# Wide cross attention on one core: the two halves of each head's queries stacked along the contraction, and the engines' order taken from a list schedule

## What is computed

```python
# x: (2, 1024, 256); context: (2, 154, 192); Wq (256, 1024), Wk, Wv (192, 1024), Wo (1024, 256), bo (256,)
n = layernorm(x)
q, k, v = n @ Wq, context @ Wk, context @ Wv      # split in 16 heads of 64
x = x + softmax(q @ k.T / 8) @ v @ Wo + bo
```

## Time and profile before

| | |
|---|---|
| median of 3 runs | 1483.45 us (1481.06 to 1484.49) |
| the profiled execution | 1474.6 us, its span from first to last instruction 1472.8 us |
| mean granted PE clock | 0.95 of full |
| busy over the span | PE 89%, PEld 70%, DVE 69%, ACT 60%, POOL 32% |
| the wide cross attention's block | 367 to 652 us of the span |

### The profile page before, as it was taken

The page is one execution under the profiler, slowest core; times in us unless marked ns, Lnnn a source line. Parts: engine busy times, 40 slices in busy tenths (PEclk is TensorE's granted clock), DMA queues, the critical chain, the costliest instruction groups (busy, mean ns, idle before and its releaser), DMA issues. The chain is left out here.

```text
span 1472.8 us, 27606 instructions
## 1 busy us (share of the span) xinstructions
PE 1311.2 (89%) x9707; PEld 1036.3 (70%) x9707; DVE 1016.0 (69%) x1992; ACT 877.4 (60%) x2193; POOL 465.7 (32%) x636
## 2 busy tenths in 40 slices
PE   5989999988699999968999766689989699999997
PEld 3534444435699999856888644478877599999995
DVE  5688787816456665555777896678875588888773
ACT  4436676674466666544121466477872588888873
POOL 5312221238233333432000356422110234444320
PEclk9999999999999999988999887599998799999998
DMA  4745224000000000021000300021202567777855
GB/s 88 225 77 155 45 53 76 6 5 1 30 2 1 2 2 1 2 93 29 1 1 1 81 16 1 22 56 42 50 16 76 176 215 230 236 233 231 232 161 184
DMA packets 97922, 116.16 MB, mean 79 GB/s; under 512 B 23552, under 2 KB 83193, under 8 KB 97785
## 3 DMA queue, kind: packets, MB, share of 16 engines
q1 hardware_dynamic: 88329, 99.84, 25.1%
q0 software_dynamic: 4416, 12.06, 2.7%
q10 hardware_dynamic: 5040, 2.49, 0.7%
HBM read 88.48 MB, written 16.55 MB: 71 GB/s over the span
## 5 line engine op out<-in xcount | busy, mean ns | idle before, releaser
L827 ACT ACTIVATE sa_probs<-ps 128x512 f32<-128x512 f32 (+1 forms) x304 | 154.3, 578 | 84.3 <-PE ps L780 83.2
L851 DVE TENSOR_REDUCE sa_top<-ps 128x2 f32<-128x1024 f32 (+3 forms) x160 | 171.4, 1115 | 37.7 <-PE ps L756 24.2
L3150 ACT ACTIVATE room<-ps,cx_top 128x154 f32<-128x154 f32 x256 | 97.2, 389 | 89.8 <-DVE cx_top L3214 89.8
L2688 PE MATMUL ps<-me_h,me_w_parts 128*128 128x256 f32 x1104 | 141.4, 289 | 4.2 <-DVE me_h L2774 4.2
L2688 PEld LDWEIGHTS ps<-me_h,me_w_parts 128*128 128x128 f32 x1104 | 138.0, 194 | 5.9 <-DVE me_h L2774 4.8
L2702 PE MATMUL ps<-me_w_parts,me_mid 128*128 128x256 f32 x1104 | 136.3, 283 | 0.0
L2702 PEld LDWEIGHTS ps<-me_w_parts,me_mid 128*128 128x128 f32 x1104 | 132.5, 188 | 0.0
L3012 POOL TENSOR_TENSOR room<-room 128x512 f32<-128x512 f32 x64 | 66.7, 1043 | 169.9 <-DVE room L3222 169.8
L2769 DVE TENSOR_TENSOR me_w_parts<-me_chunk,me_w_parts 128x1024 fp32r<-128x1024 f32 x92 | 110.4, 1222 | 13.2 <-ACT me_w_parts L2730 13.2
L2753 ACT ACTIVATE me_full<-ps,me_b 128x256 f32<-128x256 f32 x184 | 95.2, 517 | 40.5 <-PE ps L2688 40.5
L2798 DVE TENSOR_TENSOR me_mid<-me_full,me_mid 128x256 fp32r<-128x256 f32 x184 | 90.1, 507 | 41.3 <-ACT me_mid L2755 39.2
(11 more groups left out here) (472 smaller groups left out, 3437.0 us busy)
## 6 DMA issues: line engine op xcount, KB each, us to landing
me_chunk<-in_L_ffn_W_dram SPq DMA_DIRECT2D x92, 512.0 KB, 4.0
sa_k<-scr_k SPq DMA_DIRECT2D x48, 128.0 KB, 4.2
sa_q<-scr_q SPq DMA_DIRECT2D x96, 64.0 KB, 4.0
cn_qd<-cn_qh SPq DMA_DIRECT2D x60, 64.0 KB, 2.1
scr_q<-room SPq DMA_DIRECT2D x6, 512.0 KB, 4.3
scr_k<-room SPq DMA_DIRECT2D x6, 512.0 KB, 4.7
me_b<-in_L_ffn_b_dram SPq DMA_DIRECT2D x23, 128.0 KB, 4.3
x<-in_x_dram SPq DMA_DIRECT2D x4, 512.0 KB, 6.3
```

What stands on the lines that cost most here:

```text
L827: act.activation(probs[:, step % self.PROBS, h0:h0 + many, 0:w], src[:, :, 0:w], ACT.Exp, scale=DH ** -0.5).then_inc(exped.sem, 1)
L851: dve.tensor_reduce(top2[:, k % 2, k0 // 512, h0:h0 + many, sb % HBLK], src[:, :, 0:w], AX.X, ALU.max).then_inc(freed.sem, 1)
L2688: last = pe.matmul(ps[:, MID + n % 4, 0:RT], w[:, u % 2, 0, i, DM * k + P * b:DM * k + P * b + P], h[:, u % 2, j, k, :], start=(m == 0), s ...
L3150: last = act.activation(p[:, h + i, :], ps[:, S_BANK + n % SR, M * i:M * i + M], ACT.Exp, bias=top[:, t % 2, h + i:h + i + 1], accum_out=d ...
```

## The change

The query parts of two heads are no longer the stationary operand together. After each round, four DMAs of 128 KB from SP copy `cx_qh` and `cx_ql` into a new buffer `qq`, where a head owns 128 partitions: its high part in one half and its low part in the other. The keys of a head stand in both halves of `kh` and `kl`; `project_out` fills the second half by eight DMAs of 308 KB from SP, in two sets of four, and the memsets to zero go. `scores` has then two matmuls of 154 columns a head (with kh and with kl; low times low comes in too), four for a group of two heads. `qh` and `ql` shrink to one round, so `high_q` and `low_q` of a round wait for the copies of the round before. `xh` and `xl` shrink to one pair. `load_ffn` comes behind the copies of the first pair on SP. The order of PE, ACT, DVE and POOL comes from `order()`, which places each step at the earliest start by a table of durations. What `weigh`, `turn`, `output` and `exp` compute is as before.

```diff
+                for i in range(2):
+                    for keys, name in ((cross.kh, k_high), (cross.kl, k_low)):
+                        sp.wait_ge(name.sem, name.at(MB // 2 * (i + 1)))
+                        for a in range(2):
+                            own, other = W * a, W * (1 - a)
+                            part = lambda at: raw(keys[at:at + W, H // 2 * i:H // 2 * (i + 1), :, :]).rearrange(
+                                "p (m a) b k -> p a m (b k)", a=2)[:, a, :, :]
+                            sp.dma_start(part(other), part(own)).then_inc(cross.k_set[i].sem, 16)
...
-                pool.memset(cross.kh[:, :, :, :, :].bitcast(F32), 0.0).then_inc(k_zero.sem, 1)
-                pool.memset(cross.kl[:, :, :, :, :].bitcast(F32), 0.0).then_inc(k_zero.sem, 1)
...
-                act.wait_ge(k_zero.sem, k_zero.at(1))
                 for m in range(MB):
                     act.wait_ge(kmm.sem, kmm.at(m + 1))
                     for j in range(HB):
-                        last = act.activation(cross.kh[W * j:W * j + W, :, m, j, :],
+                        last = act.activation(cross.kh[W * j:W * j + W, HB * m + j, :, :],
...
-                dve.wait_ge(k_zero.sem, k_zero.at(2))
...
-        self.kh = sb("kh", [P, B, self.blocks, self.hb, M], F32R)
-        self.kl = sb("kl", [P, B, self.blocks, self.hb, M], F32R)
+        self.kh = sb("kh", [P, H, B, M], F32R)
+        self.kl = sb("kl", [P, H, B, M], F32R)
+        self.k_set = [c.own_sig(f"{name}k_set{i}") for i in range(2)]
...
+    def order(self):
+
+
+        ns, act_turns, turns = self.ns, (1, 3), self.TURNS
+        work, last = {}, {}
+
+        def add(item, engine, span, after):
+            kind = item[0], engine
+            work[item] = engine, span, after + ([last[kind]] if kind in last else [])
+            last[kind] = item
+
+        for t in range(NT):
+            add(("normal", t, 0), "DVE", 0.4, [("turn_x", t // 2 - 2, 0)] if t >= 4 else [])
+            add(("bias", t, 0), "POOL", 0.75, [("normal", t, 0)])
+            for s in range(ns):
+                after = [("exp",) + divmod(ns * t + s - 3, ns)] if ns * t + s >= 3 else []
+                if t % PAIR == 0:
+                    after.append(("laid", t // PAIR, s // 2))
+                add(("scores", t, s), "PE", 0.31, after)
+                add(("highest", t, s), "DVE", 0.41, [("scores", t, s)])
+                add(("exp", t, s), "ACT", 0.74, [("highest", t, s)] + ([("norm", t - 1, s // 2)] if t else []))
+            for q in range(QUADS):
+                add(("inverse", t, q), "DVE", 0.1, [("exp", t, 2 * q + 1)])
+                add(("norm", t, q), "POOL", 1.4, [("inverse", t, q)] + ([("turn", t - 2, 4)] if q == 0 and t >= 2 else []))
+            for i in range(5):
+                n = 5 * t + i - 2
+                after = [("norm", t, min(turns[i], 3))] + ([("turned",) + divmod(n, 5)] if n >= 0 else [])
+                if t:
+                    after.append(("weigh", t - 1, 0 if i < 2 else 1))
+                add(("turn", t, i), "PE", 0.43, after)
+                add(("turned", t, i), "ACT" if i in act_turns else "DVE", 0.5 if i in act_turns else 0.6, [("turn", t, i)])
+            for r in range(2):
+                after = [("turned", t, i) for i in ((0, 1, 2) if r == 0 else (3, 4))]
+                if t or r:
+                    after.append(("low_o", t, 0) if r else ("low_o", t - 1, 1))
+                if t:
+                    after.append(("output", t - 1, r))
+                add(("weigh", t, r), "PE", 2.0, after)
+                add(("high_o", t, r), "ACT", 0.5, [("weigh", t, r)])
+                add(("low_o", t, r), "DVE", 0.6, [("high_o", t, r)])
+                add(("output", t, r), "PE", 1.42, [("low_o", t, r)] + ([("add", t - 1, 0)] if t and r == 0 else []))
+            add(("add", t, 0), "DVE", 0.85, [("output", t, 1), ("bias", t, 0)])
+        for g in range(NPAIR):
+            add(("turn_x", g, 0), "PE", 0.43, [("normal", t, 0) for t in (2 * g, 2 * g + 1)]
+                + ([("low_q", g - 1, 3)] if g else []))
+            add(("high_x", g, 0), "ACT", 0.5, [("turn_x", g, 0)])
+            add(("low_x", g, 0), "DVE", 0.6, [("high_x", g, 0)])
+            for r in range(4):
+                add(("queries", g, r), "PE", 1.42, [("low_q", g, r - 1) if r else ("low_x", g, 0)])
+                before = [("laid",) + divmod(4 * g + r - 1, 4)] if g or r else []
+                add(("high_q", g, r), "ACT", 0.5, [("queries", g, r)] + before)
+                add(("low_q", g, r), "DVE", 0.6, [("high_q", g, r)])
+                add(("laid", g, r), "SP", 3.8, [("low_q", g, r)] + ([("scores", 2 * g - 3, 2 * r + 1)] if g >= 2 else []))
+        hop = {"PE": 0.24, "DVE": 0.17, "ACT": 0.17, "SP": 0.0, "POOL": 0.3}
+        ahead = {}
+
+        def path(item):
+
+            if item not in ahead:
+                engine, span, _ = work[item]
+                ahead[item] = span + max([path(x) + (0.03 if work[x][0] == engine else hop[engine]) for x in next_of[item]],
+                                         default=0.0)
+            return ahead[item]
+
+        next_of = {item: [] for item in work}
+        for item, (_, _, after) in work.items():
+            for a in after:
+                next_of[a].append(item)
+        for item in reversed(list(work)):
+            path(item)
+        free, end, items = dict.fromkeys(hop, 0.0), {}, []
+        while work:
+            best = None
+            for item, (engine, span, after) in work.items():
+                if all(a in end for a in after):
+                    start = max([free[engine]] + [end[a][0] + (0.03 if end[a][1] == engine else hop[end[a][1]]) for a in after])
+                    key = start - 0.005 * ahead[item]
+                    if best is None or key < best[0]:
+                        best = key, start, item
+            _, start, item = best
+            engine, span, _ = work.pop(item)
+            free[engine] = start + span
+            end[item] = start + span, engine
+            items.append((engine, item))
+        return items
...
-        xh = sb("xh", [P, 2, KD, TOK], F32R)
-        xl = sb("xl", [P, 2, KD, TOK], F32R)
-        qh = sb("qh", [P, 2, MB, TOK], F32R)
-        ql = sb("ql", [P, 2, MB, TOK], F32R)
+        xh = sb("xh", [P, KD, TOK], F32R)
+        xl = sb("xl", [P, KD, TOK], F32R)
+        qh = sb("qh", [P, 2, TOK], F32R)
+        ql = sb("ql", [P, 2, TOK], F32R)
+        qq = sb("qq", [P, 2, H, TOK], F32R)
...
-        V_AT = ((4, 0, 0), (7, 0, 1)) if wide else ((0, 1, 0),)
-        OUT_AT = ((2, 1, 1), (6, 0, 0)) if wide else ((3, 1, 0),)
-        ADD_AT = 3 if wide else 4
-        Q_AT = (2, 6) if wide else (3,)
...
-                weights.load_ffn(sp)
+                for g in range(NPAIR):
+                    for r in range(QR):
+                        if g >= 2:
+                            sp.wait_ge(s_s.sem, s_s.at(NS * (PAIR * g - 3) + 2 * r + 2))
+                        for src, swap, name in ((qh, 0, s_qh), (ql, 1, s_ql)):
+                            sp.wait_ge(name.sem, name.at(QR * g + r + 1))
+                            for a in range(2):
+                                at = 64 * (a ^ swap)
+                                dst = raw(qq[at:at + 64, g % 2, 4 * r:4 * r + 4, :]).rearrange("p (m a) n -> p a m n", a=2)
+                                sp.dma_start(dst[:, a, :, :], raw(src[64 * a:64 * a + 64, :, :])).then_inc(s_laid.sem, 16)
+                    if g == 0:
+                        weights.load_ffn(sp)
...
-                    m, h, hn = groups[s]
+                    _, h, hn = groups[s]
                     b, g, i = t // ST, t // PAIR, t % PAIR
-                    if s == 0 and i == 0:
-                        pe.wait_ge(s_ql.sem, s_ql.at(QR * g + QR))
+                    if t == 0 and s % (NS // 2) == 0:
+                        half = self.k_set[s // (NS // 2)]
+                        pe.wait_ge(half.sem, half.at(16 * 4))
+                    if i == 0:
+                        pe.wait_ge(s_laid.sem, s_laid.at(64 * (QR * g + s // 2 + 1)))
                     if n >= SR:
                         pe.wait_ge(s_exp.sem, s_exp.at(n - SR + 1))
-                    j = h - HB * m
-                    for k, (a, v) in enumerate(((qh, self.kh), (ql, self.kh), (qh, self.kl))):
-                        last = pe.matmul(ps[:, S_BANK + n % SR, 0:M * hn], a[:, g % 2, m, P * i:P * i + P],
-                                         v[:, b, m, j:j + hn, :], start=(k == 0), stop=(k == 2))
+                    for j in range(hn):
+                        for keys in (self.kh, self.kl):
+                            last = pe.matmul(ps[:, S_BANK + n % SR, M * j:M * j + M], qq[:, g % 2, h + j, P * i:P * i + P],
+                                             keys[:, h + j, b, :], start=(j == 0 and keys is self.kh),
+                                             stop=(j == hn - 1 and keys is self.kl), skip_group_check=True)
...
```

(56 more changed lines are left out.)

176 lines of the change are left out of this document (55 added, 121 removed).

## The result

| | kernel before | changed kernel |
|---|---|---|
| median of 4 runs each | 1482.45 us (1481.06 to 1484.49) | 1472.9 us (1472.02 to 1473.29) |
| ratio, 95% interval | | 0.994 (0.992 to 0.996) |
| the profiled execution, its span | 1474.6, 1472.8 us | 1473.29, 1471.6 us |
| first key product to last output, in the profiles | 351.67 to 649.79 = 298.12 us | 354.12 to 645.71 = 291.59 us |

The changed kernel is 9.5 us faster. The two profiled executions differ by only 1.3 us, because that of before was some 8 us faster than its own timed runs.

What follows compares the result with a forecast made beforehand. PE's work was taken to bound the steady part. Scores +1.0, order -2.9, head +3.5, tail -4.0 and boundary +1.0 summed to -1.4 us, from 1483.45 to 1482; likeliest 1475 to 1490, whole range 1462 to 1492.

Steps and rivals of the forecast that it cites:

- the planner's entry: Order's duration table: a group of scores has 0.31 us where 0.45 was expected; said to do PE no harm.
- The bound: Steady part, tiles 2 to 14: PE's work sets the time, 16.02 us per tile, 0.33 of it gaps.
- Scores: Score matmuls on PE: weight loads set the pace, 0.113 us each; +0.06 us per tile, +1.0 in all (-1.3 to +6.6).
- Rival 1: Score matmuls: columns set the pace, 0.07 us each, 1.19 us less per tile; whole 1462 us; chance 0.22.
- The order: Steady part: the list schedule closes gaps, leaving 0.15 us per tile; -2.9 us in all (0 to -5.3).
- Copies: Query copies: landing in 2.3 us, a round taking 4.8 us, hidden in the steady part.
- The head term: Start of the block: first scores earlier, but pair 0's last queries later through the copy chain; +3.5 us (0 to +6).
- The tail: End of the block: better order cuts PE's idle time, 14.6 us chain instead of 18.9; -4 us (-6 to 0).
- The boundary: Before the first scores: last key copies issued after the last reciprocal, memsets' removal no gain; +1.0 us (+0.3 to +1.3).
- Rival 2: Query copies are the bound: landing takes 4.2 us, a round 6.8, delaying pairs 0 and 1; +10, 1492 us; chance 0.18.
- rival 3: Steady part: the order closes no gaps, which stay at 0.33 us per tile; +2.9, 1485 us; chance 0.08.
- The likeliest case: Whole kernel: the forecast's own terms together, -1.4 us (-8 to +7), 1482 us within 1475 to 1490; chance 0.52.

Runs made afterwards that it cites:

- e6: e5 plus waits: a round's split waits for the previous round's copies, scores for their tile's copies, and the order is planned with these waits; 1473.1 us, ratio 0.9939.
- e5: e1 plus the four 128 KB query copies per round, into a buffer nobody reads; 1462.8 us, ratio 0.9873 to the kernel before.
- e11: The changed kernel, unedited, timed again on another occasion; 1476.44 us, ratio 0.9969 to the kernel before.
- e1: The kernel before with only the list-scheduled order and two finer waits, without new products or copies; 1464.5 us, ratio 0.9885.
- e9: The changed kernel with the dropped, unused 32 bytes per partition (`bq`) allocated again; 1474.02 us, ratio 0.9952 to the kernel before.
- e10: e1 with the unused 32 bytes per partition (`bq`) left out; 1464.61 us, ratio 0.9893 to the kernel before.
- e8: The changed kernel with 0.45 instead of 0.31 us for a group of scores in the planner's table; 1472.56 us, ratio 0.9937.
- e7: The changed kernel with two buffers for split queries instead of one, and next-stage weights loaded after the last copy; 1470.76 us, ratio 0.9926.
- e3: The changed kernel with score products over 128 instead of 154 columns, leaving out the last 26 keys; 1476.77 us, ratio 0.9964.
- e2: The changed kernel's data, copies and products with the hand-written order of the kernel before; 1491.82 us, ratio 1.0063.
- e4: The changed kernel with a group's four products reordered so no neighbours share a stationary operand; 1475.37 us, ratio 0.9948.

## Why the prediction was right or wrong

By the blocks: order 264.00 - 281.74 = -17.7; waits for the copies, e6 - e5, +6.3; all else, changed - e6, +3.6; and the copies of keys at the boundary +1.4. Together -6.5, the stretch's own difference (-3.5 in e11). That they add up proves nothing, since e5 and e1 have the same block and each step starts where the last ends; what counts is where each part lies. The +3.6 are 1.0 in the middle, 1.5 in the tail and 1.1 in the head. The middle's are no more than the 32 bytes (1.05 in e9, 1.21 in e10). The tail's go with the planner's entry, for e8, which has it right, is at e6's tail (41.82 and 41.74). The head's go with the clock: 2 x 0.23 x 39.07 = 18 us at the lower level against 2 x 0.18 x 37.98 = 14. The products leave no cost of their own that can be told from nothing. Point by point:

- **The bound** held. PE's work sets the time, and what PE waits for at the ends.
- **Scores.** The mechanism was right: within a group the load sets the pace, 0.112 measured for 0.113. The term, +0.06 per tile, measured 0.01 (e7 against e10), inside its bounds; 32 x 0.112 = 3.58, +0.15 per tile, would be too much, as it leaves out what happens at a group's ends. One step was a misreading: "with a transpose behind 0.07" is, in rows 4, the time from the transposes' own load (1019.27) to their first matmul (1019.34), not between two matmuls; behind a score matmul the transposes start 0.113 later here. Rival 1 leaned on the same 0.07; it is out by the distances and by e3. The 107 ns of the Trainium skill (TensorE: Matmul & The Clock Gate, section LDWEIGHTS), as 32 x 0.107 = 3.42, would give no change per tile. The distances in a group are larger, 112 ns, while the sum over the middle comes out at no change.
- **The order.** This term was mis-sized, and it is the miss. I left 0.15 us of gaps per tile; e1 leaves none, -4.5 us over the 12 tiles of the middle, where I had -2.2. And I gave the order no part in the head, apart from counting rounds up to 400: e1 shows 10.1 us less there, 5.2 at equal work. Its first score comes 10.7 us behind the first transpose of x (370.35 to 381.07), that of the kernel before 16.6, because two rounds of queries instead of four stand ahead of it and it waits for its own round alone. Together the order was to give -2.9 in the steady part and -4.0 in the tail, and it gave -17.7.
- **Copies.** Landing (2.4 against 2.3) and the first score were right: forecast 378.4 - 368.05 = 10.4 us behind the first transpose, measured 10.95. As a price of waiting, +6.3 is just beyond the upper end of +3.5 (0 to +6). That their traffic costs nothing, unsaid in the forecast, was shown by e5. The head term had the wrong sign only because the order's -10.1 was missing from it: 39.07 - 43.33 = -4.3 instead of +3.5.
- **The tail.** -4.0 forecast, 43.26 - 46.19 = -2.9 measured, -3.1 in e1. In bounds, but by luck of the cut: the changed kernel's tail holds 36 matmuls more besides the scores, 12 of `output` and a `weigh`, some 3.5 us, and at equal work it is -6.4, beyond the bound of -6. PE's idle time there fell from 8.6 to 3.1 us, where -4 was taken off 8.8. It is the order's alone: e2, with the old order, keeps 46.20.
- **The boundary.** +1.0 forecast, +1.36 measured, just beyond the upper bound of 1.3. The mechanism was right: the last pair of issues starts with the last reciprocal and takes 1.25 us, and the block's first transpose comes that much later. The memsets gave nothing back, as said (16.38 us with and without, e1).
- **Rival 2**, a landing of 4.2, is out; **rival 3**, an order that closes no gaps, too. The likeliest case had the mechanisms of scores, copies and boundary right, and the order's effect too small; its sum was -1.4 for -9.5 by the medians, -6.5 by the stretch. Its lower end of -8 was too near because the order was given no gain in the head. The 15.9 us per tile that it named as a sign of being right were met with 15.96, but in part by chance: no gaps left (15.64 in e1), plus 0.1 for the 32 bytes and 0.16 for the work that moved into the stretch.
- **What was not in it**: the 32 bytes (1.0 us), the wrong entry's 2 us in middle and tail, which the prediction called harmless to PE, and heads that differ by 3 us from one execution to the next.

## What to carry to other kernels

Before a change of several parts, list which part can act on which stretch, the ends too: here 13 of the order's 17.7 us lay in head and tail, and the forecast had given the head to the copies alone. When two orders are compared between the same two steps, count what has run between them: here 2 to 5 us of work had only crossed a cut in four of the comparisons. Count short matmuls by their weight loads: a third fewer columns in a third more matmuls, each at 0.11 us, changed the steady part by 0.1 us in 189, and a copy that a chain waits for costs time although its bandwidth is free. Try the parts one at a time: the order without the new products is 8 to 12 us faster than the change as a whole.

## What the runs showed of the hardware

Thirty-two bytes in where the tiles lie made matmuls of 256 columns 0.120 instead of 0.117 us apart, reversibly (e9, e10): with 48 such matmuls per tile, a layout can be worth 0.1 us per tile without any instruction changed. A stream of 71 GB/s between partitions left twelve tiles of matmuls at 187.68 us (e5). Score matmuls of 128 rows and 128 weight columns start 0.112 us apart with 154 moving columns and with 128, and with the stationary operand repeated or alternating (e3, e4). And the same program found its head 3.2 us longer in one execution than in another, with a mean granted clock of 0.67 instead of 0.77 there (e11).
